# Ten matmuls that nobody reads ahead of the sums over spans, in six passes of a fused block

## The reference, cut to what matters

```python
# x: 16 sequences x 256 tokens x 128; six modulation vectors per sequence from L0_c
h = layernorm(x) * (1 + ca) + sa
x = x + ga * mamba_like(h)        # in-projection, 4-tap conv, silu, selective scan, gate, out-projection
h = layernorm(x) * (1 + cb) + sb
x = x + gb * moe(h)               # shared SwiGLU (width 938) + top 2 of 8 experts of the same width

# the scan: delta = softplus(x_dbl[..., :1]); A_bar = exp(delta * A); B_bar = delta * B
h_t = A_bar_t * h_{t-1} + B_bar_t * x_t ;  y_t = h_t . C_t
```

## Time and profile before

| | |
|---|---|
| median of three runs | 744.22 us |
| the profiled execution's own time | 742.37 us |
| its span, first to last instruction | 740.6 us |
| PE busy | 651.5 us (88%) |
| DVE busy | 550.7 us (74%) |
| ACT busy | 440.0 us (59%) |
| POOL busy | 397.0 us (54%) |
| mean granted clock of TensorE | 0.94 of full |

### The profile page before, as it was taken

The page is one execution under the profiler, slowest core; times in us unless marked ns, Lnnn a source line. Parts: engine busy times, 40 slices in busy tenths (PEclk is TensorE's granted clock), DMA queues, the critical chain, the costliest instruction groups (busy, mean ns, idle before and its releaser), DMA issues.

```text
span 740.6 us, 12188 instructions
## 1 busy us (share of the span) xinstructions
PE 651.5 (88%) x3026; PEld 501.9 (68%) x3026; DVE 550.7 (74%) x1220; ACT 440.0 (59%) x804; POOL 397.0 (54%) x329
## 2 busy tenths in 40 slices
PE   4778989889998989878778999999999999999960
PEld 1555766667675667656556877877878878777840
DVE  5787988989798997987565776677776667666752
ACT  4647666685767668563444666666666666666640
POOL 2424564738456464826245847567439448472560
PEclk9688989999899999998889999999999999999995
DMA  8303111202112020211331324241320414211407
GB/s 260 78 1 102 50 50 37 64 28 75 39 57 57 29 57 28 82 32 65 108 129 44 114 78 150 66 145 52 122 72 30 157 40 122 99 49 65 135 30 232
DMA packets 47381, 59.83 MB, mean 81 GB/s; under 512 B 8756, under 2 KB 34856, under 8 KB 47360
## 3 DMA queue, kind: packets, MB, share of 16 engines
q1 hardware_dynamic: 41600, 46.91, 20.9%
q0 software_dynamic: 5760, 12.67, 4.9%
HBM read 40.01 MB, written 20.84 MB: 82 GB/s over the span
## 4 chain that ended last, share of the span: by engine, by line
PE 51%; DVE 30%; issue 10%; ACT 2%; DMA 2%; POOL 2%; DVEq 1%; SPq 1%; POOLq 0%; ACTq 0%
PE PS L671 48%; PE PS L674 4%; DVE al L1322 4%; DVE acc L1335 3%; DVE prod L1315 2%; DVE dB L1359 2%; DVE yT L1425 1%; DVE wd L1408 1%; DVE PS L1315 1%; DVE h L1447 1%; DMA yT<-result_dram 1%; DVE stats_a L1299 1%; DVE diag L1412 1%; DVE stats_b L1299 1%; DVE nx_b L1434 1%
## 5 line engine op out<-in xcount | busy, mean ns | idle before, releaser
L1034 ACT ACTIVATE sg<-PS 128x512 f32<-128x512 f32 x216 | 128.7, 597 | 131.9 <-PE PS L671 121.7
L671 PE MATMUL PS<-xh,w_lo 128*128 128x512 f32 x405 | 176.1, 435 | 13.2 <-DVE prod L1315 10.4
L1315 DVE TENSOR_TENSOR PS<-PS,sg 128x512 f32<-128x512 f32 (+1 forms) x160 | 111.3, 697 | 91.7 <-PE PS L671 60.6
L671 PE MATMUL PS<-xl,w_hi 128*128 128x512 f32 x405 | 163.8, 404 | 0.0
L671 PE MATMUL PS<-xh,w_hi 128*128 128x512 f32 x405 | 163.4, 404 | 0.0
L547 POOL DMA_INDIRECT sorted_dram<-h,slot x64 | 73.4, 1147 | 93.0 <-DVE slot L1524 66.9
L671 PEld LDWEIGHTS PS<-xh,w_lo 128*128 128x128 f32 x405 | 78.4, 194 | 46.1 <-DVE prod L1315 16.4
L609 POOL DMA_INDIRECT result_dram<-y_rows,aux_d x84 | 83.0, 989 | 37.5 <-issue 20.1
L1042 ACT CAST ah<-PS 128x512 fp32r<-128x512 f32 (+1 forms) x160 | 93.0, 581 | 15.4 <-DVE PS L1315 13.3
L671 PE MATMUL PS<-ah,w_lo 128*128 128x512 f32 x216 | 93.7, 434 | 8.1 <-ACT ah L1042 4.3
L1322 DVE TENSOR_TENSOR al<-PS,ah 128x512 fp32r<-128x512 f32 x140 | 95.7, 684 | 3.4
(11 more groups left out here) (199 smaller groups left out, 1153.1 us busy)
## 6 DMA issues: line engine op xcount, KB each, us to landing
xin<-sorted_dram SPq DMA_DIRECT2D x20, 516.0 KB
stage<-in_w_gu SPq DMA_DIRECT2D x18, 448.0 KB
sorted_dram<-pad SPq DMA_DIRECT2D x9, 516.0 KB
h<-mods_dram SPq DMA_DIRECT2D x32, 128.0 KB, 6.2
stage<-in_w_dn SPq DMA_DIRECT2D x9, 448.0 KB
tab<-mods_dram SPq DMA_DIRECT2D x8, 384.0 KB, 3.4
out<-X SPq DMA_DIRECT2D x8, 256.0 KB, 5.1
stage<-result_dram SPq DMA_DIRECT2D x6, 256.0 KB, 4.2
```

The source lines that it names most:

```text
L671: return nc.tensor.matmul(out, lhsT, rhs, start=start, stop=stop, **k)
L1034: A.activation(dst, src, ACT.Silu).then_inc(s["silu_done"], 1)
L1315: V.tensor_tensor(product_in(where, c)[0:n, :], bank("up", where, c)[0:n, :], sg[0:n, c % 3, :], ALU.mult).then_inc(s["prod_done"], 1)
```

## The change

In passes 1 to 6 PE issues ten more matmuls between `up` 6 and `sum_spans`, ahead of the wait for `delta_ready`. Each multiplies the router's high weights (`gate_hi`, 8 columns, stationary) with 128 columns of `xh` (moving), and writes 8 rows by 128 columns of PSUM bank 2, columns 384 to 511, which nothing reads. They carry no semaphore and wait for none. That is 60 matmuls in all. `sum_spans(0)` and the one of pass 0 stay as they were.

```diff
+            def keep_warm(n):
+
+                for _ in range(n):
+                    mm(PS[0:E, 2, 512 - P:512], gate_hi[:], xh[:, 0:P])
+
-            def sum_spans(g):
-
+            def sum_spans(g, filled=False):
+
+                if filled:
+                    keep_warm(10)
                 pe.wait_ge(s["delta_ready"], g + 1)
@@
                 if head:
-                    sum_spans(g + 1)
+                    sum_spans(g + 1, prev)
                 if prev:
                     up(0, g - 1, 7, NARROW)
                     down(0, g - 1, 5, NARROW)
```

## The result

| | before | changed |
|---|---|---|
| median of six runs | 744.2 us | 741.27 us |
| lowest and highest | 743.5 to 744.67 | 739.15 to 741.96 |
| profiled execution: time, span | 742.37, 740.6 | 741.73, 739.9 |
| mean granted clock | 0.940 | 0.954 |

The ratio is 0.9953 with a 95% interval of 0.9936 to 0.9971: 2.9 us less, where 1.05 us less was forecast, and just under the low end of the range (741.4). Of all the runs in this document one, of 1272.21 us, was slow; it belongs to the kernel with pass 6 written out and no pause, and the ratio leaves it out.

A forecast was written before the change was run, and what follows sets the result against it. PE, busy for 88% of the span, was taken as the main path, though it stops for DVE where changed. 742.37 less 1.05 gives 741.3; with 1.85 for the median, 743.15, forecast as 743.2 us; range 741.4 to 745.2.

The forecast's parts named there:

- Part 1: On PE ahead of `sum_spans`, passes 1 to 6: ten added matmuls take 0.65 us, with ends at 0.58 and 1.1.
- Part 2: PE's 0.97 us stop ahead of `up` 7 absorbs the ten: cost 0, or 0.4 us where cover is gone.
- Part 3: Passes 1, 3, 5: clock drops behind `sum_spans` go, 1.35 us; 0.75 if new ones come; gain taken as 1.05 us.
- The first falls: Clock drops to 0.50 just behind `sum_spans` in passes 1, 3 and 5, expected to go, worth 0.45 us each.
- the second ones: Clock drops about 10 us later in the same odd passes, worth 0.20 us each, which might go too.
- Part 4: Last passes, behind the loop: work arrives about 1 us earlier; effect taken as 0, with 1.7 us to either side.
- the full gain: Odd passes' clock drops all go, none replace them; last passes lose at most one stretch: -1.95 to -3.65 us; chance 0.25.
- The clock does not answer: Odd passes' clock drops stay and the ten cost 0 to 0.4 us: 744.2 to 744.6 us; chance 0.22.
- Slower: Clock drops move into the last passes at 330 to 400 us, up to 1.7 us per stretch; chance 0.08.

The follow-up runs named there:

- twenty: Twenty matmuls of 128 columns in place of the changed kernel's ten, at the same place: 741.77 us, ratio 0.9956.
- The kernel with 8 columns: Changed kernel with its ten added matmuls at 8 moving columns each in place of 128: 744.7 us, ratio 0.9996.
- the pause in the changed kernel: Changed kernel with pass 6 written out, plus 28 PE matmuls and two DVE zero writes ahead of y's gating: 742.96 us, ratio 0.9988.
- ten behind: Changed kernel with its ten matmuls moved behind the sums over spans, ahead of `up` 7: 740.61 us, ratio 0.9943.

## Why the prediction was wrong

- **Part 1, the price: right.** 0.60 us for ten against 0.65, 0.06 each. The estimate from the Trainium skill's figure, 0.56 us (page "TensorE: Matmul & The Clock Gate", section "Wait — 56ns, not 53.3ns?"), is as near; the measurement decides for 0.60.
- **Part 2, the cover: right.** The stop went from 0.97 to 0.32 us and ends with DVE; nothing was paid. Even twenty cost 0.3 us over five passes.
- **Part 3, the clock in the loop: right in its mechanism, nearly in its size.** The first falls of passes 1, 3 and 5 went, and the second ones with them; three new ones came, as feared, in other places. Two of them stand at the router of an even pass, as the prediction had named for pass 2. Five passes gained 1.22 us, where I took 1.05 for six, and the sums follow one another after 42.4 to 42.6 us, as written. The kernel with 8 columns shows that it is the streaming.
- **Part 4, the last passes: the step that failed.** I took 0 and kept 1.7 us to either side; it was a gain of 2.07 us, in code that was not changed. I had read one stretch at half clock there, and there were four, 23.9 us in all: 0.88 over the whole stretch, on a piece where the chain is PE for long runs. I did not put the whole of it into the argument. The experiments bear this out: of the eleven traces without fillers there, only three others show 97.3 us or more, and none shows more time at half clock. So 0 was not the middle of what could come, and a clock of 0.88 in a piece bound by PE for long runs should have told me so. How much of it would come was luck all the same: the trace before did not tell where the falls would meet the moved work. With -2.07 in that term the sum is 742.37 - 1.05 - 2.07 = 739.25, and 741.1 on the median's scale.
- **The rivals.** The time lies in the span of *the full gain* (742.3 down to 740.6), but not as told: new falls did come in the loop, and the last passes lost three stretches at half clock, not one. *The clock does not answer* fell: between 96.6 and 99.4 PE was never still for more than 0.97 us, and 0.6 us of streaming there kept the clock. The Trainium skill, page "TensorE: Matmul & The Clock Gate", section "HAM oscillation — how this bites in real kernels", speaks of gaps without any work; this trace doesn't agree with it as a full account of when the clock is lost. *Slower* names a real mechanism: the pause in the changed kernel, itself with pass 6 written out, moved the last passes from 95.4 to 97.3 us. The change happened to move them the other way.

**What stays open.** Why writing pass 6 out gains: its last passes are 1.85 us shorter than the kernel before's, which is most of its 2.6 us, but in the changed kernel they are only 0.3 us shorter (95.41 against 95.68) and the ratios' intervals overlap. Nor do the runs say what sets where the falls first come in an execution. The last passes are known from one trace of each kernel, and the runs of one kernel differ by up to some 6 us; how often each of them has the pattern of its trace is not known.

## What to carry to other kernels

Where PE waits for another engine in a passage of small matmuls, look at the granted clock of the stretch behind it; filling the wait with matmuls that stream many columns cost nothing here up to the wait's length and kept the clock, while short ones did not. Don't fill every wait for that reason alone: the kernel with fillers in the loop's other stops had more clock and was no faster. Count every stretch at half clock in the whole trace before pricing such a change, above all those where PE is the chain: work that is merely moved in time can gain or lose as much there as at the place that is changed. And give each experiment that moves work a control with the same code and no move.

## What I had not expected of the hardware

- A matmul with 8 stationary and 128 moving columns counted for the clock: ten of them, 0.60 us, kept 2.4 GHz behind the sums, while ten with 8 moving columns, 0.27 us, did not.
- Time at half clock is worth very different amounts by its place. The five passes took 212.53 us with five stretches of 3.4 us at half clock (the changed kernel with pass 6 written out) and 212.46 with two (ten behind); in the kernel before five stretches and the end of a sixth, of which three stood behind the sums, went with 213.73.
- A pause, 1.5 us more in the loop, made one kernel 4.0 us slower and left another's time where it was or 1.1 us lower.
